# Attention and expert kernel: probability tiles per key block, value products in pairs, later slots and scatters

## What is computed

```python
x = x + attn(layernorm(x))       # 16 heads of 16 channels, rotary q and k, causal softmax, output projection
x = x + ffn(layernorm(x))        # top 2 of 8 experts, each token's prob-weighted sum of two expert rows
# routing inside ffn, for every batch:
logits = x @ router_w + router_b;  top-2;  pos = cumsum(one_hot)  # place of the token at its expert
expert_inputs = zeros(E, 153, C).at[expert, pos].add(x)           # at most 153 tokens of a batch per expert
o = silu((t @ w_c_fc + b) * (t @ w_gate + b)) @ w_c_proj + b      # 8 * 153 = 1224 rows per expert
```

## Time and profile before

| what | value |
|---|---|
| median of three runs | 1281.28 us (1278.86 to 1283.59) |
| the profiled execution: its own time, its span | 1272.76 us, 1271.0 us |
| PE, DVE, ACT, POOL busy, share of the span | 93%, 58%, 38%, 54% |
| one body (2 to 6), start to start | 63.1 us |
| body 7 | 51.6 us |
| end of attention proper, first expert product | 538 us, 551.9 us |

### The profile page before, as it was taken

One profiled execution on the slowest core, in us unless ns is written; L12 is line 12 of the kernel. 1 busy time (PEld: TensorE's weight loads), 2 busy tenths in 40 slices (PEclk: granted clock), 3 DMA queues, 4 the chain that ended last, 5 costly groups with the idle time before them and its releaser, 6 DMA issues.

```text
span 1271.0 us, 24010 instructions
## 1 busy us (share of the span) xinstructions
PE 1176.4 (93%) x8264; PEld 1002.1 (79%) x8264; DVE 731.0 (58%) x1523; ACT 483.7 (38%) x988; POOL 689.9 (54%) x976
## 2 busy tenths in 40 slices
PE   4699999999999999878999999999999999999992
PEld 3466767666767676578899999999999999999982
DVE  6677787878787867755343433343433333435664
ACT  2145454545454545533333322333332233332320
POOL 4234335353535343577567655566666555767634
PEclk9699999999999999989999999999999999999996
DMA  4876745454545455343121121131211221205345
GB/s 136 219 240 189 236 118 166 118 166 121 162 122 161 121 145 127 136 138 101 63 68 59 60 71 67 65 109 59 68 59 62 75 70 64 101 26 175 100 148 177
DMA packets 83134, 148.24 MB, mean 117 GB/s; under 512 B 9647, under 2 KB 60728, under 8 KB 78910
## 3 DMA queue, kind: packets, MB, share of 16 engines
q1 hardware_dynamic: 65344, 111.37, 30.5%
q0 software_dynamic: 7936, 26.60, 6.4%
q10 hardware_dynamic: 9728, 8.67, 2.2%
HBM read 93.05 MB, written 53.61 MB: 115 GB/s over the span
## 4 chain that ended last, share of the span: by engine, by line
PE 48%; issue 2%; POOL 1%; DMA 1%; DVE 0%; POOLq 0%; DVEq 0%; ACT 0%
PE ps L77 47%; PE ps L1307 1%; POOL wp_lo L1635 1%; POOL wp_hi L1635 0%; DMA raw<-x_rows 0%; DMA wp_lo<-slot_outputs,row_of 0%; DVE raw L1504 0%; DVE xl L1375 0%; POOLq L1655 0%; DVE ah L1463 0%; DVE gated L1532 0%; DVE al L1472 0%; DVEq L1655 0%; DVE o_sb L1519 0%; POOLq L1635 0%
## 5 line engine op out<-in xcount | busy, mean ns | idle before, releaser
L1570 POOL TENSOR_TENSOR al<-hid,ah 128x384 fp32r<-128x384 f32 (+1 forms) x168 | 179.3, 1067 | 210.8 <-DVE ah L1463 210.8
L1424 ACT ACTIVATE fc<-ps,b_fc 128x384 f32<-128x384 f32 (+1 forms) x192 | 115.5, 602 | 447.6 <-PE ps L77 445.3
L1532 DVE SCALAR_TENSOR_TENSOR gated<-ps,b_gate,fc 128x384 f32<-128x384 f32 (+1 forms) x192 | 123.3, 642 | 227.3 <-PE ps L77 211.8
L824 DVE TENSOR_REDUCE mx<-ps 128x2 f32<-128x256 f32 (+3 forms) x256 | 205.9, 819 | 36.6 <-PE ps L437 34.8
L437 PE MATMUL ps<-kst,qst 65*128 65x256 f32 (+2 forms) x512 | 148.5, 373 | 11.1 <-DMA kst<-qk_parts 11.1
L606 ACT ACTIVATE probs<-ps 128x512 f32<-128x512 f32 (+1 forms) x256 | 123.1, 538 | 55.3 <-PE ps L455 54.4
L1519 DVE TENSOR_TENSOR o_sb<-ps,b_proj 128x256 f32<-128x256 f32 x80 | 33.9, 424 | 156.8 <-PE ps L77 156.8
L598 ACT ACTIVATE probs<-ps 128x256 f32<-128x256 f32 (+1 forms) x128 | 62.6, 490 | 136.2 <-PE ps L449 135.3
L958 POOL TENSOR_TENSOR rope_c<-qk_b,rope_table 128x512 f32<-128x512 f32 x32 | 43.0, 1344 | 125.7 <-ACT qk_b L634 125.6
L1392 ACT ACTIVATE hid<-gated 128x384 f32<-128x384 f32 (+1 forms) x192 | 102.7, 535 | 6.9 <-DVE gated L1532 6.9
L77 PE MATMUL ps<-xh,wg_hi 128*128 128x384 f32 (+1 forms) x384 | 103.4, 350 | 2.1 <-DVE gated L1532 2.1
(11 more groups left out here) (188 smaller groups left out, 2468.5 us busy)
## 6 DMA issues: line engine op xcount, KB each, us to landing
qk_parts<-hilo SPq DMA_DIRECT2D x32, 512.0 KB, 3.1
qst<-qk_parts SPq DMA_DIRECT2D x64, 256.0 KB, 4.9
kst<-qk_parts SPq DMA_DIRECT2D x64, 256.0 KB, 5.5
slot_tokens<-zeros POOLq DMA_DIRECT2D x12, 816.0 KB, 5.9
rows<-slot_tokens SPq DMA_DIRECT2D x24, 384.0 KB, 3.6
slot_outputs<-o_sb SPq DMA_DIRECT2D x72, 128.0 KB, 1.7
raw<-in_wf SPq DMA_DIRECT2D x8, 1024.0 KB, 5.4
raw<-in_wg SPq DMA_DIRECT2D x8, 1024.0 KB, 7.4
```

Of the source, the lines that this page charges most:

```text
L824: V.reduce_max(mx[:, g % 2, 2 * pr:2 * pr + 2, i], both[:, :, 0:P * (i + 1)], AXX)\
L1424: A(fc[:, hc % 2, 0:width], ps[:, FC + hc % 2, 0:width], ACT.Identity, bias=b_fc[:, e, hc:hc + 1]).then_inc(fc_out, 1)
L1532: V.scalar_tensor_tensor(gated[:, hc % 2, 0:width], ps[:, GATE + hc % 2, 0:width], b_gate[:, e, hc:hc + 1], fc[:, hc % 2, 0:width], ALU.ad ...
L1570: G.tensor_tensor(al[:, at, 0:width], hid[:, hc % 2, 0:width], ah[:, at, 0:width].bitcast(F32), ALU.subtract).then_inc(al_done, 1)
```

## The change

- `probs` becomes four tiles, one for each key block, each as wide as its block needs; an exponential now waits for the product of the same block one group earlier.
- `pv` for blocks 0 and 1 runs in slot 5, one after the other, and for blocks 2 and 3 in slot 1 of the next group.
- The M pieces of groups 1 and 2 move from slot 0 to slot 2, with ACT's copy and SP's send one slot behind them.
- `slots(chain, b, 1)` moves from (2, 1) to (3, 1) in bodies up to 7; it stays in body 8 and later.
- The scatters of a batch move to the next body, at (0, 5), (0, 6), (1, 3) and (1, 4), for bodies 3 to 8; the last two batches keep the old places. `hn` and `put_at` get two buffers, `st_tok` becomes two semaphores.
- SP's load of `xr` moves from (1, 4) to (0, 1), POOL's bias from (2, 1) to (0, 7).
- Ahead of `load_rows(0, 0, 0)` SP waits for the scatters of the first six batches, where it waited for `h_done`.

```diff
-        probs = sb("probs", [P, 2, GH, T])
+        probs = [sb(f"probs{j}", [P, GH, T - P * j]) for j in range(TT)]
...
-            (1, 0): ("M", 0), (1, 1): ("Q", 0), (1, 3): ("A", 0), (1, 4): ("Q", 1), (1, 5): ("F", 0),
+            (1, 1): ("Q", 0), (1, 2): ("M", 0), (1, 3): ("A", 0), (1, 4): ("Q", 1), (1, 5): ("F", 0),
...
-            (2, 0): ("M", 0), (2, 1): ("Q", 3), (2, 3): ("A", 0), (2, 4): ("V", 0), (2, 5): ("T", 0),
+            (2, 1): ("Q", 3), (2, 2): ("M", 0), (2, 3): ("A", 0), (2, 4): ("V", 0), (2, 5): ("T", 0),
...
+        def slots_at(b):
+            return (3, 1) if b < BATCH else (2, 1)
+        SCATTER_NEXT = ((0, 5), (0, 6), (1, 3), (1, 4))
+        SCATTER_LAST = ((2, 1), (2, 3), (2, 4), (2, 6))
...
-                if (g, u) == (1, 4) and there(b, 1, 8):
+                if (g, u) == (0, 1) and there(b, 1, 8):
                     wait(sp, o_out, 2 * (b - 1))
                     sp.dma_start(xr[:], ...)
...
-                        if u in (3, 5, 7) and (not isinstance(b, int) or 0 <= s - 2 <= 31):
-                            pv(s - 2, b - (g < 2), (g - 2) % 4, (u - 3) // 2)
+                        if u == 5 and (not isinstance(b, int) or 0 <= s - 2 <= 31):
+                            pv(s - 2, b - (g < 2), (g - 2) % 4, 0)
+                            pv(s - 2, b - (g < 2), (g - 2) % 4, 1)
                         if u == 1 and (not isinstance(b, int) or 0 <= s - 3 <= 31):
+                            pv(s - 3, b - (g < 3), (g - 3) % 4, 2)
                             pv(s - 3, b - (g < 3), (g - 3) % 4, 3)
...
-                        wait(act, pv_done, 4 * t + j - 1)
+                        wait(act, pv_done, 4 * t + j - 3)
...
-                if (g, u) == (2, 1) and there(b, 2, 9):
+                if (g, u) == slots_at(b) and there(b, 2, 9):
                     slots(chain, b, 1)
...
-                if (g, u) == (2, 1) and there(b, 1, 8):
+                if (g, u) == (0, 7) and there(b, 1, 8):
                     wait(pool, ld_xr, 16 * b)
                     G.tensor_tensor(xr[:], xr[:], bo_all[:]...)
...
-                if (g, u) in SCATTER_AT and there(b, 2, 9):
+                if (g, u) in SCATTER_NEXT and there(b, 3, BATCH):
                     for n in range(2):
-                        scatter(b, 2 * SCATTER_AT.index((g, u)) + n)
+                        scatter(b - 1, 2 * SCATTER_NEXT.index((g, u)) + n)
+                if (g, u) in SCATTER_LAST and there(b, BATCH, 9):
+                    for n in range(2):
+                        scatter(b, 2 * SCATTER_LAST.index((g, u)) + n)
...
             sp.wait_ge(rt["pv_done"], 4 * NG * BATCH)
-            sp.wait_ge(rt["h_done"], BATCH - 1)
+            for landed in rt["st_tok"]:
+                sp.wait_ge(landed, 16 * NB * (BATCH // 2 - 1))
             load_rows(0, 0, 0)
```

More of the change, by code:

```diff
@@ L157, in attention_phase @@
         raw_v = Region(nc, (late.at, late.end)).take("raw_v", [P, CK, C])
-        hn = late.take("hn", [P, TT, C])
+        hn = Region(nc, (late.at - 4 * CK * C * 2, late.end)).take("hn", [P, 2, TT, C])
         x_in = early.take("x_in", [P, TT, C])
@@ L190, in attention_phase @@
         base = kept.take("base", [P, 1])
-        put_at = kept.take("put_at", [P, TT * K], I32)
+        put_at = kept.take("put_at", [P, 2, TT * K], I32)
         dlt = kept.take("dlt", [P, TT])
@@ L205, in attention_phase @@
         ld_max = sem("ld_max")
-        st_zero, st_tok = sem("st_zero"), sem("st_tok")
+        st_zero = sem("st_zero")
+        st_tok = rt["st_tok"] = [sem(f"st_tok{i}") for i in range(2)]
         made, z_ready = sem("made"), sem("z_ready")
@@ L241, in attention_phase @@
         }
+        M_AT = tuple(next(u for gg, u in PIECES if gg == g and PIECES[gg, u][0] == "M") for g in range(NG))
         V_AT = ((2, 4), (3, 5))
@@ L465, in pv @@
                 for h in range(GH):
-                    last = mm(pvb[32 * h:32 * h + DH + 1, P * j:T], v_sb[:, bt % 2, j, GH * g + h, :], probs[:, j % 2, h, P * j:T],
+                    last = mm(pvb[32 * h:32 * h + DH + 1, P * j:T], v_sb[:, bt % 2, j, GH * g + h, :], probs[j][:, h, :],
                               start=(j == 0), stop=(j == TT - 1))
@@ L604, in exps @@
                     if pr == 0 and hh == 0:
-                        wait(act, pv_done, 4 * t + j - 1)
-                    A(probs[:, j % 2, 2 * pr + hh, P * j:T], ps[:, banks2(u)[hh], P * j - q0:T - q0], ACT.Exp,
+                        wait(act, pv_done, 4 * t + j - 3)
+                    A(probs[j][:, 2 * pr + hh, :], ps[:, banks2(u)[hh], P * j - q0:T - q0], ACT.Exp,
                       scale=float(DH) ** -0.5).then_inc(exp_done, 1)
@@ L616, in body_slot @@
                 s = 4 * b + g
-                if u == 1 and piece_there(b, g, "M"):
+                if u == M_AT[g] + 1 and piece_there(b, g, "M"):
                     max_out(b, g)
@@ L775, in slots @@
                 chain(V.tensor_copy(rt["slot"][:, bass.ts(b - 2, TT * K)], slot_f[:].rearrange("p t k -> p (t k)")))
-                V.tensor_tensor(put_at[:].rearrange("p (t k) -> p t k", k=K), slot_f[:], over[:], ALU.add)\
+                wait(dve, st_tok[b % 2], 16 * 8 * ((b - 2) // 2))
+                V.tensor_tensor(put_at[:, b % 2].rearrange("p (t k) -> p t k", k=K), slot_f[:], over[:], ALU.add)\
                     .then_inc(put_done, 1)
@@ L853, in body_slot @@
                     wait(dve, rs2_done, b)
[L854 to L856 removed]
+                    wait(dve, st_tok[(b - 1) % 2], 16 * 8 * ((b - 1) // 2))
+                    wait(dve, hT_done, 2 * (b - 2))
+                    normalise(hn[:, (b - 1) % 2], x1, mv2, rs2, h_done)
             def body(b):
@@ L986, in scatter @@
                     wait_apart(pool, put_done, b - 1, pool_passed)
-                G.indirect_dma_start(out=rt["tok"], out_offset=bass.IndirectOffsetOnAxis(ap=put_at[:, n:n + 1], axis=0),
-                                     in_=hn[:, n // K, :], in_offset=None, bounds_check=NSLOT - 1, oob_is_err=False)\
-                    .then_inc(st_tok, 16)
+                G.indirect_dma_start(out=rt["tok"], out_offset=bass.IndirectOffsetOnAxis(ap=put_at[:, b % 2, n:n + 1], axis=0),
+                                     in_=hn[:, b % 2, n // K, :], in_offset=None, bounds_check=NSLOT - 1, oob_is_err=False)\
+                    .then_inc(st_tok[b % 2], 16)
             def fill(n):
```

16 lines of the change are left out of this document (6 added, 10 removed).

## The result

| | kernel before | changed kernel |
|---|---|---|
| median, 20 runs each | 1281.89 us (1274.42 to 1284.18) | 1285.05 us (1279.05 to 1289.37) |
| ratio of times, 95% interval | 1 | 1.003 (1.0015 to 1.0044) |
| profiled execution (span) | 1272.76 us (1271.0) | 1284.12 us (1282.3) |

The change costs 0.3%, where 0.5% of gain was forecast (1274.3 us, range 1263 to 1283). The profiled execution of the kernel before is faster than any of its 20 timed runs, that of the changed kernel an ordinary one: the two traces differ by 11.3 us, the medians by 3.2. Where the other 8 us lie isn't shown, since there is one trace of each. So I take mechanisms from the traces and prices from the medians, and compare bodies 3 to 5 wherever I can, which stand at full clock in all traces but those of e2, e4, e5, e11 and e12.

The account below looks back on a forecast made before the run. PE was taken to set the pace, with DVE near enough to take over in places. A gain of 15.0 us in attention less 8.0 at the hand-over made 7.0, from 1281.3 to 1274.3 us, range 1263 to 1283.

Parts of the forecast that it names:

- Value products in pairs: Attention bodies: each joined run saves 0.19 us of PE's work, 12.2 us over the 32 groups.
- Slots, bias and scatters: Around (2, 1): with bias and chain gone, PE's waits of 1.25 us ahead of (2, 4) and 0.24 ahead of V go.
- A body by parts: One body divided at Q, V and M: 2.0 - 0.6 + 1.3 = 2.7 us gained.
- M through the next body to Q: From M of (3, 0) to the next body's Q of (1, 4), 38.1 us: -1.3, bounds 0 and -2.6.
- Q to V: From Q of (1, 4) to V of (2, 4), 17.05 us: -2.0 from fewer runs and waits, bounds -1.0 and -2.2.
- Bodies 3 to 6: Four attention bodies, each gaining 2.7 us: 10.8 together.
- Body 2: Body without scatters, where POOL's bias follows the inverse root at once and lies on `xn`: 2.0 us gained.
- Body 7: Body of 51.6 us without X, Q and V: 1.3 us gained, nearly the run overheads alone.
- Body 0: First attention body: 0.5 us gained.
- The scatters of the last batches: Hand-over to the experts: POOL's 27.3 us chain in body 8 delays the rows, first product 8 us later, bounds 5 and 10.
- The rival that the scatters collide with `xn`: At (0, 5) and (0, 6): scatters lengthen `xn` by 3.8 us, 2.9 a body, giving 1286 us; chance 0.12.
- The base: Whole kernel: difference reckoned on the profiled 1272.8 us, then applied to the median of 1281.3, 8.5 higher.

Follow-up runs that it names:

- e2: Kernel before with the joined value products alone (four tiles of probabilities), nothing moved: 1292.28 us, ratio 1.0077 to the kernel before.
- e4: e2 with the M pieces of groups 1 and 2 moved from slot 0 to slot 2: 1292.69 us, ratio 1.0085 to the kernel before.
- e5: e1 with both joined runs one slot earlier, at the ends of slots 4 and 0: 1290.07 us, ratio 1.0104 to the kernel before.
- e11: e3 with each maximum taken over only the first half of its keys: 1331.77 us, ratio 0.9979 to the kernel before.
- e12: e8 with each maximum taken over only the first half of its keys: 1309.58 us, ratio 0.9842 to the kernel before.
- e3: Kernel before with the moves of slots, bias and scatters alone, first expert rows waiting only for batches 0 to 2: 1278.45 us, ratio 0.9986.
- e6: e3 with products 0 and 1 joined in slot 5: 1276.32 us, ratio 0.9971 to the kernel before.
- e7: e3 with products 2 and 3 joined in slot 1: 1289.03 us, ratio 1.0074 to the kernel before.
- e8: e3 with both joins, M at its old places: 1283.69 us, ratio 1.0030 to the kernel before.
- e1: Changed kernel with the first expert rows' load waiting only for the scatters of batches 0 to 2: 1281.27 us, ratio 1.0001 to the kernel before.
- e16: e13 with products 0 and 1 joined in group 1 too: 1274.35 us, ratio 0.9939 to the kernel before.
- e13: e6 with products 0 and 1 apart in group 1 and the bias waiting for the normalisation: 1271.00 us, ratio 0.9925 to the kernel before.
- e17: e1 with the bias waiting until the normalisation is done: 1277.01 us, ratio 0.9969 to the kernel before.
- e9: e6 with products 0 and 1 apart in group 1 and that group's M in slot 2: 1315.90 us, ratio 0.9873 to the kernel before.

## Why the prediction was wrong, point by point

- **Value products in pairs**: right as PE's work (12.2 forecast, 12.3 measured).
- **Slots, bias and scatters**: right in kind; alone they give 1.6 us a body (e3). `over` at (3, 1) took 1.17 us, forecast at most 1.3, and no longer holds PE.
- **A body by parts**, medians of bodies 3 to 5, in us (sum: -2.7 forecast, -0.84 measured):

| part | before | forecast | measured |
|---|---|---|---|
| Q of (1, 4) to V of (2, 4) | 17.05 | -2.0 | -1.45 |
| V to M of (3, 0) | 7.93 | +0.6 | +0.86 |
| M to V of (3, 5) | 10.98 | +0.3 | +0.41 |
| V of (3, 5) to M of (0, 0) | 5.00 | -0.26 | -0.08 |
| M of (0, 0) to the maximum of (0, 5) | 8.35 | -0.96 | -0.86 |
| maximum of (0, 5) to Q of (1, 4) | 13.79 | -0.35 | +0.28 |

- **M through the next body to Q** is the step that failed: -1.3 forecast, -0.25 measured, 1.0 of the 1.8 us that a body falls short. It was reckoned on VectorE's side. Up to (0, 5) it is 0.4 short (-0.5 for -0.9); the term that failed outright, in its sign, is that from there to Q "the joined blocks gain 0.35". They cost there: against e3's 13.91 us this part is 0.28 longer with the first join (e6), 0.37 with the second (e7), 0.69 with both (e8), and the move of M gives 0.53 back (e1). I had seen that VectorE is nearly always busy there, but not that in slots 5 and 1 it waits for PE, so that a product put ahead of its scores is paid. "From M of (3, 0) to V of (3, 5) it is +0.3" was the only place where I charged product 2; e7 has +0.42, +0.38 and +0.43 in groups 1, 2 and 3.
- **Q to V** went the same way: of its two joined runs I counted only what they save. The run of (1, 5) costs 0.87 there (15.14 in e16, 14.27 in e13), and I had a wait of 1 us at Q(1, 4) on the list of signs but not in the sum.
- **Bodies 3 to 6** together: 10.8 of gain forecast, 3.9 measured.
- **Body 2**, forecast 2.0 of gain: 0.8 of loss. I had written that the bias "lies on `xn`" and then priced it at 0.7. It costs 2.05 us of VectorE and with it 1.6 of the body (63.9, and 62.3 in e17). And it does not follow the inverse root at once: it waits for the load of `xr`, of which I wrote that it costs nothing, issued "ten places" ahead. From (0, 1) to (0, 7) it is six, and the bias could start only 6.2 us after SP issued the load.
- **Body 7**: 1.3 of gain forecast, 0.7 of loss. It is the second join again: from `x1` of body 6 to `x1` of body 7 it is 51.7 us before, 51.8 in e3, 51.1 with the first join (e6) and 52.9 with the second (e7).
- **Body 0**: 0.5 of gain forecast, 2.2 of loss. PE waits 2.5 us for a maximum and stays at 1.2 GHz 3.4 us longer. No run ties this to an edit; e1 and e17, which do the same in body 0, differ there by 1.5 us (54.9 and 53.4).
- **The scatters of the last batches**: the chain of 27.3 us was right (27.5, from 520.37 to 547.88), and the first product came 8.8 us late for 8.0, or 9.2 with the 0.3 that attention gained. That the absolute times fit so well (549.36 for 549.2) is in part luck: I had taken them from the old timeline, as if attention gained nothing. What I missed is the second client of GpSimd's queue, the inverse root for the last `hn`, which takes back over half when the rows are freed.
- **The rival that the scatters collide with `xn`** is refuted: 1.43 to 1.59 us beside four scatters, 1.37 without. It had the right place and the wrong instruction: the bias collides.
- **The base**: an offset of 8.5 us from a fast profiled execution to the median was added as if both kernels had it; the changed kernel's is 0.9.

What remains open: the last body with scatters and splits in another order, so that neither the rows nor the last inverse root stand behind sixteen scatters. It was not tried. That early rows take back a part of the cost is shown by e1; that `rs` holds the rest is read from its timeline alone.

## What to carry to other kernels

- A piece of work on one engine has a price by its place: free in a slot where that engine waits for the other, full price where the other waits for it. Before moving one, list for each slot who waits for whom; the starts of the second engine's regular instructions give it in one column.
- A saving in each of 64 places may be a gain in some and a loss in others. Here the first join kept in three groups of four, the second dropped, the early rows and the wait of the next point together took a change of +0.3% to -0.75%.
- An instruction that is kept from a collision only by timing needs a wait of its own. One wait was worth 0.3% in two pairs of runs (e1 and e17, e6 and e16); each pair ran on two chips, and the intervals of its ratios just touch. And when work is pushed into the last body, follow everything that its queue still has to do, not only the first to wait.

## What the runs showed of the hardware

- VectorE's four normalising instructions take 1.37 us alone, 1.37 to 1.62 beside GpSimd's scatters, and 2.2 to 4.3 beside a GpSimd `tensor_tensor` of 1024 columns (2.4 us), by how far the two overlap and what stands beside them. "SBUF — State Buffer" of the Trainium skill, Who interferes with whom, has the port pair as a lock held for a whole instruction; the bias rows agree. The scatters' rows show hardly any hold.
- Waits of PE of 1.9 to 3.0 us in the attention stage were followed by stretches at 1.2 GHz: 3.4 us behind 2.0 (e2), 1.9 (e6) and 2.5 (e3), 10.2 us behind 2.6 (e7) and behind 3.0 and 2.1 (e5). A stretch of 10.2 us at half speed takes up to 5.1 us more, which is above the wait itself.
- The same kernel, the one before, has medians of 1279.3 to 1281.9 us in five series and 1331.8 in the one that ran on the chip of e9 to e12.
